# A two-projection adapter on one core: single register loads for the first loads of x, and TensorE's up projection of the last tile but one ahead of the last down projection

## The reference

```python
h = einsum('bsh,bhk->bsk', x, W_down[itok]) + b_down[itok]     # 512 -> 256
h = gelu(h)                                                    # exact gelu
h = einsum('bsk,bkh->bsh', h, W_up[itok]) + b_up[itok]         # 256 -> 512
h = x + h
mean, var = mean(h), mean((h - mean)**2)                       # over the 512
out = (h - mean) * rsqrt(var + 1e-5) * ln_w[itok] + ln_b[itok]
```

## Time and profile before

| | |
|---|---|
| median of 3 runs | 135.51 us |
| the profiled execution | 135.53 us, of it a span of 133.8 us |
| TensorE busy | 126.1 us (94%), weight loads 113.6 us |
| VectorE busy | 112.6 us (84%) |
| GpSimd busy | 105.4 us (79%) |
| ScalarE busy | 85.2 us (64%) |
| mean DMA rate | 164 GB/s |

### The profile page before, as it was taken

How to read it: one execution, slowest core, us unless ns; L and a number is a source line. 1 busy time by engine, 2 the same in 40 slices (tenths; PEclk the granted TensorE clock), 3 DMA queues, 4 the chain that set the end, 5 groups by cost and what they waited for, 6 DMA issues and landing times.

```text
span 133.8 us, 4073 instructions
## 1 busy us (share of the span) xinstructions
PE 126.1 (94%) x850; PEld 113.6 (85%) x851; DVE 112.6 (84%) x276; ACT 85.2 (64%) x179; POOL 105.4 (79%) x119
## 2 busy tenths in 40 slices
PE   6997999999999999999999999999999999999840
PEld 6896979899999999899999999999999999998620
DVE  1798696988879999988888888988888978888995
ACT  0757687666665797666666667666666666666610
POOL 7001957999879997998888888888888889999851
PEclk9999999999999999999999999999999999999999
DMA  1968876995665554544555556545455655331376
GB/s 39 339 198 252 267 207 171 330 290 157 168 186 163 174 151 138 151 145 121 150 138 149 160 154 157 157 157 157 157 157 157 157 157 119 79 77 31 68 196 182
DMA packets 13249, 21.95 MB, mean 164 GB/s; under 512 B 2345, under 2 KB 3890, under 8 KB 13234
## 3 DMA queue, kind: packets, MB, share of 16 engines
q1 hardware_dynamic: 8850, 15.74, 40.0%
q10 hardware_dynamic: 4384, 6.05, 16.2%
HBM read 13.39 MB, written 8.65 MB: 165 GB/s over the span
## 4 chain that ended last, share of the span: by engine, by line
PE 90%; DVE 6%; DVEq 1%; issue 1%; ACT 0%
PE hg_ps L921 35%; PE y_ps L954 32%; PE xT_ps L906 11%; PE xT_ps L865 5%; PE hg_ps L931 5%; PE y_ps L875 2%; DVE r_stats L732 1%; DVE res L781 1%; DVE y_ps L772 1%; DVEq L690 1%; DVE hb L720 1%; DVE scaled L759 1%; ACT xT_hi L481 0%; DVE r_mv L736 0%; DVE res L767 0%
## 5 line engine op out<-in xcount | busy, mean ns | idle before, releaser
L390 POOL TENSOR_TENSOR xb<-x_sb,bu_rows 128x512 f32<-128x512 f32 x33 | 43.1, 1307 | 10.0 <-DVE bu_rows L707 9.8
L407 POOL TENSOR_TENSOR res<-normed,lnb_rows 128x512 f32<-128x512 f32 (+1 forms) x31 | 39.2, 1266 | 8.0 <-ACT normed L506 7.8
L486 ACT ACTIVATE g<-hb 128x256 f32<-128x256 f32 x33 | 13.8, 419 | 32.2 <-DVE hb L720 32.2
L732 DVE BATCH_NORM_STATS2 r_stats<-y_ps 128x6 f32<-128x512 f32 x33 | 22.9, 694 | 3.4 <-issue 2.6
L921 PE MATMUL hg_ps<-wd_hi,xT_hi 128*128 x132 | 24.0, 303 | 0.9 <-ACT xT_hi L481 0.9
L712 DVE TENSOR_TENSOR xT_lo<-xT_ps,xT_hi 128x512 fp32r<-128x512 f32 x33 | 22.7, 688 | 1.9 <-ACT xT_hi L481 1.9
L954 PE MATMUL y_ps<-wu_hi,gT_hi 128*128 (+1 forms) x66 | 23.3, 433 | 0.6 <-ACT gT_hi L491 0.5
L759 DVE SCALAR_TENSOR_TENSOR scaled<-y_ps,r_mv,lnw_rows 128x512 f32<-128x512 f32 x31 | 23.1, 745 | 0.4
L506 ACT ACTIVATE normed<-scaled,rstd 128x512 f32<-128x512 f32 x31 | 22.4, 723 | 0.0
L396 POOL TENSOR_TENSOR rstd<-var_eps,half_neg 128x1 f32<-128x1 f32 x33 | 18.1, 548 | 4.6 <-DVE var_eps L741 4.3
L921 PE MATMUL hg_ps<-wd_lo,xT_hi 128*128 x132 | 21.1, 282 | 0.0
(11 more groups left out here) (89 smaller groups left out, 152.9 us busy)
## 6 DMA issues: line engine op xcount, KB each, us to landing
x_sb<-in_x_dram SPq DMA_DIRECT2D x64, 128.0 KB, 2.7
out_dram<-res ACTq DMA_DIRECT2D x33, 128.0 KB, 2.4
out_dram<-res SPq DMA_DIRECT2D x33, 128.0 KB, 2.3
wd<-in_L_cond_W_down_dram ACTq DMA_DIRECT2D x3, 512.0 KB, 4.9
wu<-in_L_cond_W_up_dram SPq DMA_DIRECT2D x6, 256.0 KB, 3.8
lnw_rows<-in_L_cond_ln_w_dram SPq DMA_DIRECT2D x1, 768.0 KB, 5.4
lnb_rows<-in_L_cond_ln_b_dram SPq DMA_DIRECT2D x1, 768.0 KB, 6.8
x_sb<-in_x_dram ACTq DMA_DIRECT2D x2, 128.0 KB, 3.1
```

What stands on the lines that cost most here:

```text
L390: pool.tensor_tensor(xb[:, c % DEEP, :], x_sb[:, c % FAR, :], bu_rows[:, ds(e * H, H)], ALU.add).then_inc(xb_ready, 1)
L407: pool.tensor_tensor(res[:, c % FAR, part], normed[:, c % DEEP, part], lnb_rows[:, ds(e * H, part.stop)], ALU.add).then_inc(res_ready, 1)
L732: dve.bn_stats(r_stats[:, c % DEEP, :], y_ps[c % YBANKS][:]).then_inc(stats_ready, 1)
```

## The change

At the front: SyncE and ScalarE load one register ahead of each of their first two loads of x, in place of four at once, and ScalarE asks for its half of x(0) ahead of its second cast of the down weights. VectorE's sort has one linked step less, and the rest of the biases (`biases_lo`) is made while VectorE waits for the key. TensorE spreads the third down bias last, multiplies ones three times and no longer five times before x(0), and does two passes of down(0) ahead of `transpose_x(1)` and one behind it, in place of one and two. ScalarE's `keep_up_bias(1)` goes behind the down biases and `gelu(0)` ahead of a cast; VectorE's copy of the third up bias goes behind `x_lo(0)`, and `x_lo(1)` behind `down_bias(0)`.

At the back: TensorE does `up(31)` ahead of `down(32)`. VectorE's `down_bias(32)` goes behind `scale_last(31)`, `g_lo(32)` behind `shift_last(31)`. ScalarE's `rescale(30)` goes ahead of `gelu(32)`, the stores of tiles 27 and later all behind `g_hi(32)`, and their places are loaded earlier.

```diff
--- before.py
+++ after.py
@@ -40,6 +40,9 @@
 
     LAST = TILES - 2
 
+    LAST_PLACES = {i: (LAST + 2 * i + 2, LAST + 2 * i + 3) for i in (-3, -2)}
+    LAST_PLACES[-1] = LAST, LAST + 1
+
     FAR = 8
     DEEP = 4
     PAR = 2
@@ -62,7 +65,7 @@
     DVE_LOWS, POOL_LOWS = (2, 3, 4), (0, 1, 2)
 
 
-    WARM_UPS = 10, 4, 5
+    WARM_UPS = 10, 4, 3
 
     with ExitStack() as ctx:
         def sb(name, shape, dt=F32):
@@ -315,9 +318,9 @@
                 return [sp.snap(reg, min_val=0, max_val=B - 1) for reg in regs]
 
             sp.wait_ge(slots_ready, 1)
-            sp.reg_load(head_regs, io_table[0:1, 0:4])
             for t in range(2):
-                load_half(sp, t, 0, sp.snap(head_regs[3 * t], min_val=0, max_val=B - 1))
+                sp.reg_load(head_regs[t:t + 1], io_table[0:1, 3 * t:3 * t + 1])
+                load_half(sp, t, 0, sp.snap(head_regs[t], min_val=0, max_val=B - 1))
             sp.wait_ge(slots_ready, 2)
             sp.reg_load(head_regs[:1], io_table[0:1, 5:6])
             load_w_up(sp, 0, slot_expert(0, head_regs[0]))
@@ -530,22 +533,23 @@
             act.wait_ge(biases_in, 32)
             act.copy(biases_hi[:], biases[:]).then_inc(biases_hi_ready, 1)
             wd_high(0)
-            head_regs = [act.alloc_register(f"act_head{i}") for i in range(4)]
+            head_regs = [act.alloc_register(f"act_head{i}") for i in range(2)]
             act.wait_ge(slots_ready, 1)
-            act.reg_load(head_regs, io_table[0:1, 1:5])
-            wd_high(1)
             for t in range(2):
-                load_half(act, t, 1, act.snap(head_regs[3 * t], min_val=0, max_val=B - 1))
+                act.reg_load(head_regs[t:t + 1], io_table[0:1, 3 * t + 1:3 * t + 2])
+                load_half(act, t, 1, act.snap(head_regs[t], min_val=0, max_val=B - 1))
+                if t == 0:
+                    wd_high(1)
             wd_high(2)
-            for e in range(E - 1):
-                keep_up_bias(e)
+            keep_up_bias(0)
             x_hi(0, 0)
             keep_down_bias(0)
             keep_down_bias(1)
+            keep_up_bias(1)
             x_hi(1, 1)
             wu_high(0, 0)
+            gelu(0, 0)
             wu_high(0, 1)
-            gelu(0, 0)
             g_hi(0, 0)
             gelu(1, 1)
             x_hi(2, 2)
@@ -598,7 +602,7 @@
                 x_hi(t + 2, c + 2)
                 rescale(t - 3, c - 3)
                 if isinstance(t, int):
-                    for n in (t + 1, t + 2) if t == TILES - EARLY - 2 else (t + 2,):
+                    for n in LAST_PLACES[t - LAST]:
                         last_places[n] = place(n)
 
             tiles(act, body, LATE + 2, TILES - 3)
@@ -612,13 +616,11 @@
             g_hi(last - 1, last - 1)
             seed(last, last)
             rescale(last - 3, last - 3)
+            rescale(last - 2, last - 2)
+            store(last - 6, last - 6)
             gelu(last, last)
-            store(last - 6, last - 6)
             g_hi(last, last)
-            rescale(last - 2, last - 2)
-            store(last - 5, last - 5)
-            store(last - 4, last - 4)
-            for t in range(last - 3, TILES):
+            for t in range(last - 5, TILES):
                 store(t, t, last_places[t])
 
         @block.vector
@@ -646,6 +648,7 @@
                 last = dve.tensor_scalar(of_expert[:, e, :], itok_all[:], float(e), None, ALU.is_equal, ALU.add,
                                          accum_out=count[:, e:e + 1])
             link(last)
+            dve.tensor_scalar(even_count[:], count[:], 0.5, TO_EVEN, ALU.add, ALU.add)
             for e in range(E - 1):
 
                 dve.tensor_scalar(behind[:, e:e + 1], itok_own[:], float(e + 1), None, ALU.is_ge)
@@ -654,14 +657,16 @@
             link(dve.scalar_tensor_tensor(out=same_before[:], in0=itok_all[:], scalar=itok_own[:], in1=before[:],
                                           op0=ALU.is_equal, op1=ALU.mult, accum_out=rank[:]))
 
-            dve.tensor_scalar(rank_code[:], rank[:], float(RANGE), code[:], ALU.mult, ALU.add)
-            link(dve.tensor_scalar(even_count[:], count[:], 0.5, TO_EVEN, ALU.add, ALU.add))
-            link(dve.scalar_tensor_tensor(out=slots_before[:], in0=even_count[:], scalar=-TO_EVEN, in1=behind[:],
-                                          op0=ALU.add, op1=ALU.mult, accum_out=ahead[:]))
+            dve.scalar_tensor_tensor(out=slots_before[:], in0=even_count[:], scalar=-TO_EVEN, in1=behind[:],
+                                     op0=ALU.add, op1=ALU.mult, accum_out=ahead[:])
+            link(dve.tensor_scalar(rank_code[:], rank[:], float(RANGE), code[:], ALU.mult, ALU.add))
 
             dve.tensor_scalar(key_col[:], ahead[:], float(RANGE), rank_code[:], ALU.mult, ALU.add)
             dve.tensor_scalar(onehot[:], slot_row[:], rank[:], ahead[:], ALU.subtract, ALU.is_equal).then_inc(
                 key_ready, 1)
+            dve.wait_ge(biases_hi_ready, 1)
+            dve.tensor_tensor(biases_lo[:], biases[:], biases_hi[:].bitcast(F32), ALU.subtract).then_inc(
+                biases_lo_ready, 1)
             dve.wait_ge(key_ready, 2)
 
             link(dve.tensor_tensor_scan(key_filled[:, 1:1 + SLOTS], key_ps[0:1, 0:SLOTS], zero_row[:], 0.0,
@@ -679,9 +684,6 @@
             dve.tensor_tensor(pair_view[:, :, 0], tile_expert[:], tile_expert[:, 0:1].broadcast_to([1, TILES]),
                               ALU.subtract)
             dve.tensor_copy(pair_view[:, 0:TILES - 1, 1], tile_expert[:, 1:TILES]).then_inc(slots_ready, 1)
-            dve.wait_ge(biases_hi_ready, 1)
-            dve.tensor_tensor(biases_lo[:], biases[:], biases_hi[:].bitcast(F32), ALU.subtract).then_inc(
-                biases_lo_ready, 1)
 
             near_regs = [dve.alloc_register(f"near{i}") for i in range(4)]
 
@@ -703,9 +705,6 @@
             dve.reg_load(first_regs, tile_expert[0:1, 0:3])
             first_experts = [dve.snap(reg, min_val=0, max_val=E - 1) for reg in first_regs]
 
-            dve.wait_ge(up_spread, E)
-            dve.tensor_copy(bu_rows[:, (E - 1) * H:E * H], y_ps[E - 1][:]).then_inc(bu_last_ready, 1)
-
             def x_lo(t, c):
 
                 dve.wait_ge(xhi_ready, t + 1)
@@ -783,9 +782,11 @@
                                          op0=ALU.mult, op1=ALU.add).then_inc(last_ready, 1)
 
             x_lo(0, 0)
-            x_lo(1, 1)
+            dve.wait_ge(up_spread, E)
+            dve.tensor_copy(bu_rows[:, (E - 1) * H:E * H], y_ps[E - 1][:]).then_inc(bu_last_ready, 1)
             dve.wait_ge(bd_ready, len(bd_banks))
             down_bias(0, 0, first_experts[0])
+            x_lo(1, 1)
             w_up_low(dve, 0, 0).then_inc(wu_lo_ready, 1)
             down_bias(1, 1, first_experts[1])
             g_lo(0, 0)
@@ -839,17 +840,24 @@
                 return near[3], near[2], near[1]
 
             tiles(dve, body, LATE, TILES - 3)
-            e_last = body(TILES - 2, TILES - 2)
-
             last = TILES - 1
+            near = experts_near(last - 1)
+            e_last = near[3], near[2], near[1]
+            stats(last - 2, last - 2)
+            g_lo(last - 1, last - 1)
+            dve.wait_ge(stats_ready, last - 1)
+            mean_var(last - 2, last - 2)
+            variance(last - 2, last - 2)
+            scale(last - 2, last - 2, near[1])
             stats(last - 1, last - 1)
             dve.wait_ge(stats_ready, last)
             mean_var(last - 1, last - 1)
             variance(last - 1, last - 1)
-            g_lo(last, last)
             shift_half(last - 2, e_last[2])
             scale_last(last - 1, e_last[1])
+            down_bias(last, last, e_last[0])
             shift_last(last - 1, e_last[1])
+            g_lo(last, last)
             stats(last, last)
             dve.wait_ge(stats_ready, last + 1)
             mean_var(last, last)
@@ -881,10 +889,11 @@
             pe.wait_ge(biases_lo_ready, 1)
             spread_row(bd_banks[0], 0, 0)
             spread_row(bd_banks[0], 1, 1).then_inc(down_spread, 1)
-            spread_row(bd_banks[1], 0, 2).then_inc(down_spread, 1)
             for e in range(E):
                 spread_row(y_ps[e], 0, E + 2 * e)
                 spread_row(y_ps[e], 1, E + 2 * e + 1).then_inc(up_spread, 1)
+            pe.wait_ge(slots_ready, 1)
+            spread_row(bd_banks[1], 0, 2).then_inc(down_spread, 1)
             expert_regs = [pe.alloc_register(f"expert{i}") for i in range(2)]
 
             next_regs = [pe.alloc_register(f"next_expert{i}") for i in range(3)]
@@ -963,9 +972,9 @@
             warm_up(WARM_UPS[2], xT_ps[1])
             transpose_x(0, 0)
             pe.wait_ge(wd_hi_ready, E)
-            down(0, 0, e_first, (0,))
+            down(0, 0, e_first, (0, 1))
             transpose_x(1, 1)
-            down(0, 0, e_first, (1, 2))
+            down(0, 0, e_first, (2,))
             pe.wait_ge(bd_ready, len(bd_banks))
             down(1, 1, e_next)
             transpose_g(0, 0)
@@ -997,7 +1006,10 @@
 
```

(5 more changed lines are left out.)

## The result

| | before | after |
|---|---|---|
| median | 135.53 us (135.37 to 135.85, 6 runs) | 138.42 us (138.01 to 139.00, 6 runs) |
| ratio, with its 95% interval | | 1.0215 (1.0191 to 1.0239) |
| the profiled execution | 135.53 us, span 133.8 | 139.00 us, span 137.2 |

A forecast was written before the change was run, and what follows sets the result against it. TensorE was taken to bound 90% of the span, VectorE the back. The sum was 135.53 - 0.15 (front) + 2.0 (back) = 137.4 us, with an 8 in 10 range of 136.5 to 138.4.

The forecast's parts named there:

- Steps (1) to (4): At the front: shorter sort, early biases_lo, fewer ones and earlier loads start the transposes of x(0) 0.6 us earlier.
- Step (5): At the front: the new pass order of down(0) gives back 0.45 us, so down(1) starts at 14.3, not 14.47.
- Step (6): At the front: bu_rows about 0.8 us later, covered by GpSimd's idle 1.58; the remaining moves cost nothing.
- The back: Last tiles: y(32) at 131.8, VectorE's end at 134.5, tile 31's landing at 135.2 to 135.4 ends the span; +2.0 us.
- Rival (a): At the back: the reorder pays, as VectorE's queue ends 0.3 us earlier; 135.1 us, chance 0.07.
- (d): At the back: the reorder costs nothing because something unseen hides down(32) again; 135.4 us, chance 0.05.
- Rival (b): The front keeps its 0.6 us and the stores at the back are quicker; 136.6 us, chance 0.12.
- rival (c): At the back: TensorE's clock falls while waiting for g(32), up(32) runs at half rate, 1.6 us more; 139.0, chance 0.08.
- Front: The start of the kernel, all edits there summed: -0.15 us, with bounds -0.35 and +0.2.

The follow-up runs named there:

- E7: The kernel before with the changed front, but bias copies, x_lo(1) and the passes of down(0) in their old order: 135.38 us, ratio 0.9973.
- E3: The kernel before with the changed front, but the up bias copies and x_lo(1) at their old places: 135.43 us, ratio 0.9991.
- E5: The kernel before with only keep_up_bias(1), VectorE's copy of the third up bias and x_lo(1) moved late: 136.79 us, ratio 1.0088.
- E6: The kernel before with the whole changed front, and GpSimd waiting for both wu_lo of VectorE ahead of xb(1): 137.21 us, one run.
- E9: The kernel before with the changed back, ScalarE's stores spread and eight matmuls of ones ahead of transpose_g(32): 137.45 us, ratio 1.0142.
- E12: E9 with VectorE's down_bias(32) ahead of shift_half(30) and scale_last(31), and four matmuls of ones: 137.84 us, ratio 1.0145 to the kernel before.
- E2: The kernel before with all of the change's edits at the back and the old front: 138.24 us, ratio 1.0174.
- E1: The kernel before with all of the change's edits at the front and the old back: 136.18 us, ratio 1.0034.
- E4: The kernel before with the changed back and eight matmuls of ones ahead of transpose_g(32): 138.06 us, ratio 1.0175.
- E11: E7 with ScalarE's last places loaded early and GpSimd waiting for both wu_lo ahead of xb(2): 135.44 us, ratio 0.9989 to the kernel before.
- E8: The kernel before with the changed back, ScalarE's stores of tiles 27 to 29 spread ahead of g_hi(32): 138.28 us, ratio 1.0187.

## Why the forecast came out 1 us too low

**Steps (1) to (4), the start of x(0): right in the main, with x(0) at the late bound.** ScalarE's ask for x(0) went out at 7.26 in place of 8.01, by a first register load of 0.48 (forecast 7.2). TensorE was ready at 9.73 and not at 10.2: the eight loads of ones ahead of the spreads took 0.97 where they had taken 1.47, which the forecast did not have and which x(0) hid. x(0) was there only at 10.49, 0.1 earlier than before. ScalarE's half did land 0.57 earlier (10.00 for 10.57), but the last one is SyncE's now: asked for at 7.28, only 0.12 earlier than before, it took 3.2 to land and not 2.65. In the other profiles with this front the last half came at 10.0 to 10.3; why it varies was not settled.

**Step (5), the passes of down(0): right.** E7 against E3 gives 0.48 from down(0) to down(1), forecast 0.45.

**Step (6), "The rest hides": this failed.** bu_rows did come 0.95 later, and GpSimd's own idle time of 1.58 did cover GpSimd: its wu_lo, at 19.39, still stood 1.23 waiting for ScalarE. What it doesn't cover is what GpSimd's additions run beside. E5 alone costs 1.17, E3 without them nothing, E6 with GpSimd silent nothing in up(0). The rows agree on one rule. VectorE's wu_lo, both of whose inputs are in SBUF, ends 0.54 to 0.56 behind the xb that was running when it was issued:

| | GpSimd's xb ends | wu_lo ends | difference |
|---|---|---|---|
| changed kernel, second wu_lo | 13.95+4.21 = 18.16 | 17.61+1.11 = 18.72 | 0.56 |
| E5, second | 14.27+4.22 = 18.49 | 17.94+1.11 = 19.05 | 0.56 |
| E7, first | 12.64+2.53 = 15.17 | 14.49+1.22 = 15.71 | 0.54 |
| kernel before, first | 14.24+1.29 = 15.53 | 15.20+0.88 = 16.08 | 0.55 |

That the difference stays the same while wu_lo's own time goes from 0.88 to 1.22 says that it is a wait and then a plain run, not a slower run. The next xb in turn waits for wu_lo: xb(2) took 1.74 in the changed kernel and 1.73 in the kernel before, and 1.28 in E9, where it began as wu_lo ended. x_lo, down_bias and g_lo, with one input in PSUM, took their 0.69 and 0.41 beside the same additions.

The Trainium skill says this on its page SBUF — State Buffer, section SBUF: two separate sides: a VectorE instruction with two SBUF inputs and a GpSimd instruction that reads SBUF take their shared ports as an exclusive lock, the first to start for its whole length, and the other blocks. The trace agrees, with the numbers above. By that rule step (6) should have been: each wu_lo now meets an xb, so each can be late by up to one xb, 1.3. The kernel before had the sign of it in its own rows: its first wu_lo took 0.88 and the second 0.68.

**The back: right in each step of the chain up to VectorE's end, wrong in what ends the span.** The chain holds within 0.1 up to up(32) in the changed kernel (the table above) and to VectorE's end in E9. Then the forecast said "the end of the span isn't that" and took tile 31's landing. It is VectorE's end, with its 1.01 behind it: by the forecast's own 134.5 the span ends at 135.5, 1.75 later than before, and in E9 at 135.46. Forecast +2.0, E9's ratio +1.9 and its profile +1.8 agree, but that the landing gave nearly the same sum is in part luck. Rival (a), that the reorder pays, is refuted by E9 and E12, and (d), that the back costs nothing, by E2. Rival (b), a front that keeps its 0.6, is refuted by E1 and E3; with the old passes E7 kept 0.47 of it at tile 1.

**The clock, a term that the sum had at nothing: this failed too.** As rival (c) it was given 0.08, and it happened in most runs. Of the six runs of E2 five had a mean granted clock of 0.977 to 0.987, of the changed kernel three of six 0.988 or less, against 0.988 at the lowest that was noted for the kernel before. The argument against it was that 2.8 us of little work is well below the 4.7 behind the earlier trace rows. That compared a case where nothing had to fall sooner with the one at hand: the 4.7 shows one idle stretch that was long enough, not how short one may be; in E2's profile the clock fell 2.3 behind the last matmul of down(32) (127.5 to 129.8). Its price, 1.6, was the upper end. In the changed kernel's profile only the end of up(32) ran at the lower level, and y(32) lost 0.5; the two groups of times are 0.9 apart. In E2's profile all of up(32) did, and y(32), at 132.18+1.06 = 133.24 less a shift of 0.18, is 1.3 behind E9's. By E9 and E4, ones in the wait keep the clock.

The Trainium skill's page TensorE: Matmul & The Clock Gate, section Part 4: PE-mode transpose, had been weighed and set aside. The two transposes indeed did not protect the clock here, as the page says; eight matmuls of ones did.

**The burst of stores was not in the forecast as a risk.** It had the stores behind g_hi(32) at the old pace, less a place load: 3.0 from the first to tile 31's. In the changed kernel this held (130.87 to 133.97 is 3.1) and the last landing did not count; in E4's profile it was 4.3, and ended the span.

**The sum, remade.** Front +0.46 (E1) in place of -0.15; the back +1.9 (E9) in place of +2.0; clock and stores together +0.4 (E2 less E9) in place of nothing: 135.53+0.46+1.93+0.43 = 138.35, measured 138.42. Of the miss of 1.0, 0.6 is step (6) and 0.4 the clock and the stores. These are differences of ratios whose intervals are 0.3 to 0.5 us wide either way; that they meet to 0.1 is better than they can be trusted. In the profiled run of the changed kernel it was the clock alone, with 0.5.

**Open:** the stalls of 0.1 to 0.45 inside the loop, when x(0) lands, what held up the stores in E4, and whether stores end any other run of the changed kernel.

## What to carry to other kernels

When a piece of work on a side engine moves, its own slack is only half the question: list what the other engines will run beside it at the new place, and whether they read the same memory by the same ports. If one instruction of a group already takes longer than its twins, look which one of another engine ends just before it does. And a matmul that fills the wait for a handover does two jobs: taken away, the wait becomes visible, and TensorE's clock may fall in it.

## What the hardware showed beyond expectation

- VectorE's instruction on two SBUF operands (0.68) waits for the end of GpSimd's running one and then takes 0.55; GpSimd's next one waits for VectorE's (1.29 becomes 1.74, and 1.85 in E11). Instructions with an operand in PSUM took their usual 0.41 and 0.69 beside it.
- TensorE's clock fell to 1.2 GHz after a stretch in which it had waited 2.0 us, done two transposes and waited 0.8 more. In E2's and E8's profiles it fell at 129.8, right behind the two transposes and 2.3 and 2.5 behind the end of down(32)'s last matmul, before up(32) began; one other run of E2 and two of E8 have a mean of 0.998 or more.
- Store issues of ScalarE, 0.48 each at rest, took up to 1.85 behind one another. A store that is skipped because its place lies beyond the batch takes 0.17, on SyncE 0.15.
- The span ended 1.01 behind VectorE's last instruction or 0.49 behind the last landing of a store, whichever was later, in fourteen profiles.
- A single register load took 0.47 to 0.49 as the first on SyncE and ScalarE, and 0.28 to 0.30 as the second.
